# Two steps per batch taken off VectorE: the residual add goes to ScalarE and GpSimd, the sort offsets to TensorE

## The chip, the cores and the metric

One core of one Trainium2 chip runs the whole program. The metric is device time in microseconds (us) of one launch; the time of a kernel is the median of its runs. Five engines work side by side and meet only at semaphores: TensorE (PE; its weight loads are PEld), VectorE (DVE), ScalarE (ACT), GpSimd (POOL) and SyncE (SP), which here only issues DMAs. Each engine executes its own instructions in the order in which the program lists them.

## The reference, cut to what matters

The input is x of shape (8, 512, 128): 8 batches of 512 tokens. The block computes

```
x = layernorm(x + attention(x) @ Wo)     # 16 heads, differential, causal, RMS per head
x = layernorm(x + experts(x))            # 8 experts; each token goes to one of them
```

The attention of a batch needs softmax over 512 keys for 32 query heads of 4 values. Routing: `logits = x @ router_w + router_b`; a token goes to the expert of the largest logit, `y = (silu(a) * g) @ w2[e]`, and y is scaled by the largest softmax probability. The change touches two places: the sum `x + attention(x) @ Wo` ahead of the first layer norm, and the arithmetic that turns a token's expert and its rank among that expert's tokens into a row number.

## The kernel before, in words

**Phases.** The attention runs in 34 phases g = 0 to 33, four per batch (`SUPER` = 4, two of the eight key heads each). A phase has 9 slots t, each with two units u = 2t and 2t + 1. In a unit, TensorE makes scores for two uses: of phase g the block whose row maxima are wanted (VectorE reduces it, `row_max`, line 1396), and of phase g - 2 the turned block, which ScalarE exponentiates (line 963) and TensorE multiplies with v (`pv`, line 756). At the end of a phase VectorE folds the maxima (`pair_max`, lines 1405 and 1406); GpSimd splits them into three bf16 parts (`split_max`, lines 1141 to 1147, the first thing of its next phase); TensorE turns them (`turn_max`, line 793, slot 2 of the next phase), and they reach a later phase by DMA.

**Banks.** Scores and all small products go through two rings of PSUM banks: three banks emptied by VectorE (`nat_b`, semaphore `s_nfree`) and four emptied by ScalarE (`st_b`, `s_sfree`). Which ring a named product uses is told by `FOR_DVE` (line 122). In the last phases, products of batch 7 use an eighth bank.

**The chain of a batch.** Behind the attention of batch b comes a chain whose steps are placed by hand in tables: `CHAIN` gives for TensorE, ScalarE and GpSimd a phase (4b + lag) and a slot, `JOBS` for VectorE a phase and a unit from which one step follows each unit. In order: GpSimd forms the difference of the heads (`over_total`, `difference`, phase 4b + 6), `square`, `inverse_root` and `rms_norm` (4b + 7), `turn_attn` (4b + 8), the product with Wo (`wo`, 4b + 9, slot 8), VectorE's residual add from the bank into `res` (line 1417), six steps `stats` on VectorE (lines 1433 and 1439), `layer_norm` on GpSimd (lines 1224 to 1229, 4b + 10, slot 3), `turn_x1` (4b + 10, slot 8), `router` (4b + 11, slot 2, line 818), `choose` on VectorE, `rank` on TensorE (lines 824 to 833, 4b + 12), `place` on VectorE (lines 1481 to 1486), and `sort` on GpSimd: four indirect DMAs that scatter the tokens to `x_sorted` (line 1241). Every engine takes its entries in program order, so the steps of different batches that fall in one phase stand in line behind each other. In phases 4b + 10, GpSimd has in this order: `split_max`, four `split` steps of the keys of batch b + 3 (lines 1124 to 1130), `layer_norm(b)`, `over_total(b + 1)` and `difference(b + 1)`; then follows `split_max` of the next phase.

**Batch 6** is the exception: `CHAIN_SHORT` and `JOBS_SHORT` press its chain into phases 32 and 33; all six of its `stats` steps are done at unit 9 of phase 32. Phase 32 also holds the `place` steps of batch 5, from unit 8 on. `jobs_at` (line 142) yields the jobs of one unit by rising batch. The last step of `place` of batches 5 and 6 also runs `group(0)` and `group(1)` (line 1510): some twenty dependent little instructions that give the experts and rows of the slots of the second part; SP waits on them for the expert weights (`s_es`) and the rows (`s_base`), and for the scattered tokens (`s_scat`).

**The second part** (after phase 33): 23 slots of up to 256 sorted tokens each, `turn_x`, `hidden`, `down` on TensorE, with `take_x`, `gate` and `mix` on VectorE; batch 7's chain is woven in between.

Of the kernel before, what the change touches and what calls it, by code (L numbers as in the profile page):

```python
# [12 lines left out]
ALU = mybir.AluOpType  # L13
# [91 lines left out]
def outs_before(j, par):  # L105
# [15 lines left out]
BATCH_USES = [(6, "q", -4), (8, "q2", -4), (2, "k", -3), (6, "k2", -3), (2, "v", -2)]  # L121
FOR_DVE = ("wo", "router", "rank")

# [12 lines left out]

JOBS = {"guess": (7, 8, 3), "stats": (9, 17, 6), "choose": (11, 6, 8), "chance": (12, 0, 2),
        "place": (12, 8, 3)}
JOBS_SHORT = {"stats": (8, 9), "choose": (9, 7), "chance": (9, 12), "place": (9, 13)}
# [41 lines left out]


def rings():

    nat, st, nat_out, st_out = {}, {}, 0, 0
    nat_at, st_at = [], []
    for g in range(PHASES):
        for t in range(NC):
            if g < NS:
                for u in (2 * t, 2 * t + 1):  # L190
                    nat["max", g, u] = len(nat_at)
                    nat_out += 1
                    nat_at.append(nat_out)
            if 0 <= g - LAG < NS:
                for u in (2 * t, 2 * t + 1):
                    st["exp", g - LAG, u] = len(st_at)
                    st_out += 1
                    st_at.append(st_out)
            for name, n in uses(g, t):
                if name in FOR_DVE:  # L200
# [14 lines left out]
def build(nc, xT, x, wq, wv, wo, lam, rms, router_w, router_b, w12, c_rope, c_sign, c_ident, c_mask, c_tri, c_iota,  # L215
          c_rows, c_pad, out):
    with ExitStack() as ctx:
# [6 lines left out]
        def sem(name):  # L224
            return ctx.enter_context(nc.semaphore(name))
# [13 lines left out]
        mask_h, turned_h = (bits[:, 2 + 2 * i:4 + 2 * i, :].rearrange("p h (n t) -> p h n t", n=2) for i in range(2))  # L239
        tri = sb("tri", [P, 2, P], BF16)  # L240
        iota = sb("iota", [P, 4 * 16 + 2 * NX + NX * NX + 5 * 16 + SLOT // P + 1 + NTILE])
# [207 lines left out]
        s_rs2 = sem("s_rs2")  # L449
        s_norm = sem("s_norm")  # L450
        s_last = sem("s_last")
        s_outs = [sem("s_outs0"), sem("s_outs1")]
# [3 lines left out]

        RT_STEPS = 12

# [14 lines left out]
        def place(name, n):  # L473

            if (name, n) in TAIL_NO:
                return pv_b, s_tail, TAIL_NO[name, n], s_tfree
            if name in FOR_DVE:
                return nat_b[NAT_NO[name, n] % NAT_RING], s_nat, NAT_NO[name, n], s_nfree
            return st_b[ST_NO[name, n] % ST_RING], s_st, ST_NO[name, n], s_sfree

        def emptied(eng, name, n):

            if (name, n) in TAIL_NO:
                eng.wait_ge(s_tfree, TAIL_NO[name, n] + 1)
            elif name in FOR_DVE:
                eng.wait_ge(s_nfree, NAT_OUT[NAT_NO[name, n]])
            else:
                eng.wait_ge(s_sfree, ST_OUT[ST_NO[name, n]])

        def batch_of(g, lag):  # L490
# [4 lines left out]
        def over(a, shape, axis):  # L495
# [12 lines left out]
                  (rw_s[:, :], router_w), (rb_s[:, :], router_b.partition_broadcast(P)),  # L508
                  (tri[:, :, :], c_tri), (iota[:, :], c_iota),
                  (row_u[:, :, :].rearrange("p j a -> p (j a)"), c_rows)]  # L510
# [43 lines left out]
        def _(sp):  # L554
# [33 lines left out]
            for g in range(PHASES):  # L588
# [16 lines left out]
                for b in range(B - 1):  # L605
                    if g == SUPER * b + (CHAIN_SHORT if b == B - 2 else CHAIN)["wo"][0] + 1:

                        emptied(sp, "wo", b)
                        sp.dma_start(xn[:, :, :], x[(b + 1) * T:(b + 2) * T, :].rearrange("(i p) d -> p i d", p=P))\
                            .then_inc(s_xn, 16)  # L610
# [50 lines left out]
        def _(pe):  # L661
# [121 lines left out]
            def use(name, n):  # L783
                bk, done, no, _ = place(name, n)
                if (name, n) in TAIL_NO:
                    wait(pe, s_tfree, no)
                elif name in FOR_DVE:
                    nat_wait(pe, no)
                else:
                    st_wait(pe, no)  # L790
# [30 lines left out]
                elif name == "rank":  # L821
# [3 lines left out]
                    for i in range(NI - 1):  # L825
                        shape = [P, NI - 1 - i, NX]
                        m = pe.matmul(own[:, i + 1:NI, :], tri[:, 1, :], over(chosen[:, n % 2, i, :], shape, 1),
                                      start=False, stop=True, skip_group_check=True)
                    if n:
                        m = pe.matmul(own, tri[:, 1, :], over(cnt[:, n, :], [P, NI, NX], 1), start=False, stop=True,  # L830
                                      skip_group_check=True)
# [117 lines left out]
        def _(act):  # L949
# [25 lines left out]
            def take(name, n):  # L975
                if name in FOR_DVE:
                    return
# [16 lines left out]
                elif name == "turn_attn":  # L994
                    if n:
                        emptied(act, "wo", n - 1)
                    dst, src = dt_s[:, :], bk[:, :]
                elif name[0] in "qk":
                    a, cols = "qk".index(name[0]), HALF[len(name) - 1]
                    wait(act, s_split[a], 4 * n)  # L1000
                    dst, src = rot[:, a, cols], bk[:, cols]
                else:
                    if n:
                        emptied(act, "router", n - 1)
                    dst, src = x1t[:, :], bk[:, :]
# [90 lines left out]
        def _(pool):  # L1096
# [112 lines left out]
            def rms_norm(b):  # L1209
                wait(pool, s_newton, NEWTON * (b + 1))  # L1210
                wait(pool, s_post, 4 * b + 3)
                if b:
# [3 lines left out]
                    .then_inc(s_post, 1)  # L1216

            def layer_norm(b):

# [30 lines left out]
            for g in range(PHASES):  # L1250
                for t in range(NC):
# [20 lines left out]
                    if b is not None and t == 6:  # L1272
                        rms_norm(b)
                    b = chain_at("norm", g, t)
                    if b is not None:
# [51 lines left out]
        def _(dve):  # L1327
# [80 lines left out]
            def take(name, n):  # L1408
                if name not in FOR_DVE:
                    return  # L1410
# [12 lines left out]
                else:  # L1423
                    if n in GROUP_BATCH:
                        V.tensor_copy(total[:, n - GROUP_BATCH[0], :], bk[:, NI * NX:NI * NX + NX]).then_inc(s_total, 1)
                    V.tensor_tensor(coded[:, :, :], bk[:, 0:NI * NX].rearrange("p (i e) -> p i e", i=NI),
                                    over(io_region, BT, 1), ALU.add).then_inc(free, 1)

            def stats(b, k):

                if k < NI:
                    emptied(dve, "wo", b)
                    V.bn_stats(bst[:, k, :], res[:, k, :]).then_inc(s_bn, 1)
# [42 lines left out]
            def place_of(b, k):  # L1476

                wait(dve, s_rt, RT_STEPS * b + 10 + k)
                if k == 0:
                    emptied(dve, "rank", b)  # L1480
                    V.tensor_tensor(place_f[:, :, :], coded[:, :, :], chosen[:, b % 2, :, :], ALU.mult)\
                        .then_inc(s_rt, 1)
                elif k == 1:
                    V.tensor_reduce(pos_f[:, :], place_f[:, :, :], AX.X, ALU.add).then_inc(s_rt, 1)
# [360 lines left out]
```

## Time and profile before

| | us |
|---|---|
| median of 3 runs | 613.77 |
| the runs | 612.7, 620.75, 613.77 |
| profiled execution, its own time | 616.7 |
| its span, first to last instruction | 614.8 |
| PE busy | 566.8 (92% of the span) |
| DVE busy | 503.3 (82%) |
| ACT busy | 427.4 (70%) |
| POOL busy | 336.6 (55%) |
| mean granted TensorE clock | 0.950 |

The span leaves out 1.9 us of the execution's own time. Busy times of different engines overlap; a share is a mean over the attention phases and the second part, which have different limits. All the times given below are positions or lengths in this one execution.

### The profile page before, as it was taken

What the parts mean: (1) busy time and instruction counts of PE and PEld (TensorE: products, weight loads), DVE (VectorE), ACT (ScalarE), POOL (GpSimd) and SP (SyncE); (2) the same over time, 40 slices, a digit from 0 to 9 for tenths busy, and PEclk for the clock granted to TensorE, in tenths of its full rate; (3) what the DMA queues carried; (4) which work ended last, traced back from release to release, by engine and by line L of the source; (5) the groups of instructions that cost most, each with busy time, mean ns of one, the idle gap of its engine ahead of it and who ended that gap; (6) DMA issues with size and microseconds to landing.
All of it is one profiled execution on the core that took longest, in us unless ns stands there. A gap on an engine that the chain in (4) does not pass through costs nothing.

```text
span 614.8 us, 30825 instructions
## 1 busy us (share of the span) xinstructions
PE 566.8 (92%) x12925; PEld 341.1 (55%) x12925; DVE 503.3 (82%) x1251; ACT 427.4 (70%) x898; POOL 336.6 (55%) x573
## 2 busy tenths in 40 slices
PE   5499999999999999999999999999999797999992
PEld 1245454445554554455455445545555586999992
DVE  4477998998998999899989989999975688766673
ACT  3104888988887898888788888988888425444441
POOL 5322033772677397647748673842755216655584
PEclk9555899999999999999999999999999899999997
DMA  3603313321431342134124313312105682778510
GB/s 109 184 5 109 99 35 85 101 60 33 110 93 52 94 108 58 51 86 119 37 79 105 86 52 83 104 34 55 45 9 191 184 291 74 262 251 281 197 53 22
DMA packets 44083, 62.85 MB, mean 102 GB/s; under 512 B 13436, under 2 KB 35196, under 8 KB 43800
## 3 DMA queue, kind: packets, MB, share of 16 engines
q1 hardware_dynamic: 38888, 54.31, 30.2%
q0 software_dynamic: 2416, 5.08, 2.3%
q8 instruction: 102, 1.67, 1.2%
q10 hardware_dynamic: 2640, 1.48, 0.9%
q14 instruction: 37, 0.30, 0.2%
HBM read 42.79 MB, written 21.65 MB: 105 GB/s over the span
## 4 chain that ended last, share of the span: by engine, by line
PE 47%; DVE 22%; POOL 16%; issue 6%; DMA 4%; ACT 2%; SPq 0%; POOLq 0%; DVEq 0%; ACTq 0%
DVE mr L1396 15%; PE bank L756 10%; PE bank L892 8%; PE bank L689 7%; PE bank L671 6%; PE bank L907 3%; PE bank L767 3%; POOL x_all L1229 3%; PE bank L773 3%; PE bank L809 1%; PE bank L799 1%; PE bank L708 1%; DMA x_sorted<-x_all,pos_u 1%; POOL dif L1175 1%; POOL rstd L1226 1%
## 5 line engine op out<-in xcount | busy, mean ns | idle before, releaser
L1396 DVE TENSOR_REDUCE mr<-bank 128x8 f32<-128x512 f32 x576 | 363.0, 681 | 45.1 <-PE bank L689 42.5
L963 ACT ACTIVATE work<-bank 128x512 f32<-128x512 f32 x576 | 313.8, 600 | 54.8 <-PE bank L708 48.3
L756 PE MATMUL bank<-work,v_aug 128*32 128x256 f32 (+6 forms) x2560 | 172.5, 368 | 0.3 <-issue 0.3
L689 PE MATMUL bank<-kd,qd 24*64 24x192 bf16 (+7 forms) x2048 | 171.0, 295 | 0.0
L708 PE MATMUL bank<-qd,kd 27*64 27x320 bf16 (+7 forms) x2048 | 160.2, 286 | 0.0
L671 PEld LDWEIGHTS bank<-bits 32*64 32x64 bf16 x4608 | 79.3, 105 | 142.3 <-DVE mr L1396 65.3
L671 PE MATMUL bank<-bits 32*64 32x64 bf16 (+2 forms) x4608 | 134.2, 212 | 21.6 <-DMA kd<-qk_parts 10.7
L756 PEld LDWEIGHTS bank<-work,v_aug 128*32 128x32 f32 x2560 | 62.8, 109 | 57.7 <-issue 21.2
L1141 POOL CAST msplit<-mt 128x32 bf16<-128x32 f32 x32 | 6.7, 210 | 119.4 <-DVE mt L1406 119.4
L689 PEld LDWEIGHTS bank<-kd,qd 24*64 24x64 bf16 x2048 | 69.2, 111 | 0.0
L708 PEld LDWEIGHTS bank<-qd,kd 27*64 27x64 bf16 x2048 | 65.6, 108 | 0.1
L1076 ACT ACTIVATE sa<-bank 128x256 f32<-128x256 f32 (+1 forms) x92 | 30.4, 348 | 37.5 <-PE bank L892 29.0
L1241 POOL DMA_INDIRECT x_sorted<-x_all,pos_u x32 | 31.7, 992 | 27.0 <-DVE pos_u L1486 19.2
L1288 POOL DMA_INDIRECT out_dram<-ynorm,row_u x39 | 39.4, 1011 | 10.3 <-issue 8.8
L1111 POOL TENSOR_TENSOR xr<-xt_s,rope 128x512 f32<-128x512 f32 x28 | 34.7, 1271 | 9.7 <-DMA xt_s<-in_xT 9.7
L1726 DVE TENSOR_TENSOR u_s<-sa,bank 128x256 f32<-128x256 f32 (+1 forms) x92 | 32.3, 375 | 9.3 <-ACT sa L1076 8.6
L892 PE MATMUL bank<-xr,work 128*128 128x256 f32 (+1 forms) x192 | 37.2, 347 | 2.6 <-DVE xr L1682 2.5
L892 PE MATMUL bank<-xr,wbuf 128*128 128x256 f32 (+1 forms) x176 | 37.2, 365 | 1.3 <-DVE xr L1682 1.1
L892 PEld LDWEIGHTS bank<-xr,work 128*128 128x128 f32 x192 | 31.2, 191 | 6.0 <-DVE xr L1682 3.0
L1065 ACT ACTIVATE ynorm<-ymix,shift,rstd 128x128 f32<-128x128 f32 x37 | 16.5, 486 | 24.9 <-DMA out_dram<-ynorm,row_u 15.3
L892 PEld LDWEIGHTS bank<-xr,wbuf 128*128 128x128 f32 x176 | 30.3, 197 | 5.4 <-DVE xr L1682 1.7
L1298 POOL TENSOR_TENSOR rstd<-var,half 128x2 f32<-128x2 f32 (+1 forms) x23 | 15.5, 672 | 24.1 <-DVE var L1708 23.7
(203 smaller groups left out, 714.1 us busy)
## 6 DMA issues: line engine op xcount, KB each, us to landing
qk_parts<-parts SPq DMA_DIRECT2D x91, 128.0 KB, 2.6
work<-in_w SPq DMA_DIRECT2D x12, 768.0 KB, 6.3
wbuf<-in_w SPq DMA_DIRECT2D x11, 768.0 KB, 6.1
kd<-qk_parts SPq DMA_DIRECT2D x64, 96.0 KB
qd<-qk_parts SPq DMA_DIRECT2D x62, 96.0 KB
x_sorted<-in_c_pad SPq DMA_DIRECT2D x9, 390.0 KB, 4.3
xr<-x_sorted SPq DMA_DIRECT2D x16, 130.0 KB, 2.6
xt_s<-in_xT SPq DMA_DIRECT2D x8, 256.0 KB, 3.8
```

The source lines that it names most:

```text
L671: pe.matmul(bk[L * c:L * c + L, :].rearrange("p (n t) -> p n t", t=L)[:, first:first + step * (wide - 1) + 1:step, cols], unit_h[lo:lo + L ...
L689: m = pe.matmul(bk[L * c:L * c + L, cols], qd[lo:lo + KROWS, s % 2, second, c, L * n:L * n + L], kd[lo:lo + KROWS, s % 2, second, c, 0:key ...
L708: m = pe.matmul(bk[L * c:L * c + L, cols], kd[lo:lo + KROWS + MAXROWS, s % 2, second, c, L * n:L * n + L], qd[lo:lo + KROWS + MAXROWS, s % ...
L756: m = pe.matmul(pv_b[32 * t:32 * t + 32, lo:hi], v_aug[:, vb, kv + v, kb, :], prob[:, pos, r, lo - back:hi - back], start=piece == 0, stop ...
L892: m = pe.matmul(banks[f][:, h * SLOT:h * SLOT + P * WIDE[j]], w_slots[j % WRING][:, h * FFN + f * P:h * FFN + (f + 1) * P], xst[:, n % 2, ...
L963: nc.scalar.activation(prob[:, pos, r, :], st_b[no % ST_RING][:, :], ACT.Exp, scale=HD ** -0.5).then_inc(s_sfree, 1)
L1076: nc.scalar.activation(sa[:, f, 0:P * WIDE[j]], banks[f][:, 0:P * WIDE[j]], ACT.Silu).then_inc(s_silu, 1)
L1111: nc.gpsimd.tensor_tensor(xr[:, i, :], xt_s[:, :], rope[:, i, :], ALU.mult).then_inc(s_xr, 1)
L1241: nc.gpsimd.indirect_dma_start(out=x_sorted, out_offset=bass.IndirectOffsetOnAxis(pos_u[:, n:n + 1], 0), in_=x1_all[:, n, :], in_offset=None)\
L1288: nc.gpsimd.indirect_dma_start(out=out, out_offset=bass.IndirectOffsetOnAxis(row_u[:, j, a:a + 1], 0), in_=ynorm[:, j % 2, a, :], in_offse ...
L1396: V.tensor_reduce(mr[:, s % 2, u % 2, i, i:i + NB], nat_b[no % NAT_RING][:, :].rearrange("p (n t) -> p n t", t=L), AX.X, ALU.max)\
L1726: V.tensor_tensor(u_s[:, j % 2, f, 0:cols], sa[:, f, 0:cols], banks[f][:, SLOT:SLOT + cols], ALU.mult)\
```

## The change: what it does

For batches 0 to 5 the bank of the product with Wo belongs to ScalarE's ring instead of VectorE's. ScalarE copies it to `res` (128x512 f32), and GpSimd then adds `xn` to `res` in place (`add_x`, in phase 4b + 9, slot 8). SP's load of the next `xn` and VectorE's `stats` wait on the new semaphore `s_res`. The six `stats` steps of a batch begin four units later (from unit 17 of phase 4b + 9 to unit 3 of phase 4b + 10). Batches 6 and 7 keep VectorE's add.

In the ranks, one more small product on TensorE adds the region offset of each expert, so that the bank holds the whole row number; VectorE multiplies the bank by the flags `chosen` in the step that empties it. The separate addition of `io_region` goes, `place` has two steps instead of three, and `RT_STEPS` is 11 instead of 12. The constant `tri` becomes 8 columns wider.

```diff
-FOR_DVE = ("wo", "router", "rank")
+FOR_DVE = ("router", "rank")
...
-JOBS = {"guess": (7, 8, 3), "stats": (9, 17, 6), "choose": (11, 6, 8), "chance": (12, 0, 2),
-        "place": (12, 8, 3)}
+JOBS = {"guess": (7, 8, 3), "stats": (10, 3, 6), "choose": (11, 6, 8), "chance": (12, 0, 2),
+        "place": (12, 8, 2)}
...
+def for_dve(name, n):
+    return name in FOR_DVE or name == "wo" and n >= B - 2
...
+        def whole(eng, b):
+
+            if for_dve("wo", b):
+                emptied(eng, "wo", b)
+            else:
+                eng.wait_ge(s_res, b + 1)
...
-                        emptied(sp, "wo", b)
+                        whole(sp, b)
...
+                    m = pe.matmul(own, tri[:, 1, :], over(regions, [P, NI, NX], 1), start=False, stop=True,
+                                  skip_group_check=True)
...
+                elif name == "wo":
+
+                    wait(act, s_x1, 4 * n)
+                    dst, src = res[:, :, :], bk[:, :].rearrange("p (i d) -> p i d", i=NI)
...
+            def add_x(b):
+                emptied(pool, "wo", b)
+                wait(pool, s_xn, 16 * (b + 1))
+                nc.gpsimd.tensor_tensor(res[:, :, :], res[:, :, :], xn[:, :, :], ALU.add).then_inc(s_res, 1)
...
+                    b = chain_at("wo", g, t)
+                    if b is not None and not for_dve("wo", b):
+                        add_x(b)
...
-                    V.tensor_tensor(coded[:, :, :], bk[:, 0:NI * NX].rearrange("p (i e) -> p i e", i=NI),
-                                    over(io_region, BT, 1), ALU.add).then_inc(free, 1)
+                    V.tensor_tensor(place_f[:, :, :], bk[:, 0:NI * NX].rearrange("p (i e) -> p i e", i=NI),
+                                    chosen[:, n % 2, :, :], ALU.mult).then_inc(free, 1)
...
                 if k < NI:
-                    emptied(dve, "wo", b)
+                    whole(dve, b)
...
                     emptied(dve, "rank", b)
-                    V.tensor_tensor(place_f[:, :, :], coded[:, :, :], chosen[:, b % 2, :, :], ALU.mult)\
-                        .then_inc(s_rt, 1)
-                elif k == 1:
                     V.tensor_reduce(pos_f[:, :], place_f[:, :, :], AX.X, ALU.add).then_inc(s_rt, 1)
                 else:
                     V.tensor_copy(pos_u[:, NI * b:NI * b + NI], pos_f[:, :]).then_inc(s_pos, 1)
```

## Rows read from the trace of the kernel before

**Rows 1.** Windows, one batch: length; busy PE, PEld, DVE, ACT, POOL; clock, DMA, GB/s.

```profile
212.33:267.44 55.11, 53.33 (x1533) 28.45 (x1537) 50.56 (x107) 46.74 (x95) 36.49 (x63) 1.00 0.29 78
```

**Rows 2.** Chain that ended last, 214 to 219 us: start, length, what.

```profile
214.68 0.24 POOL msplit L1147
...
218.72 0.24 POOL vare L1224
```

**Rows 3.** Timeline of PE at slot 2 of phase 15: start, length, what, [idle before].

```profile
229.65 0.23 PE L793 MATMUL bank<-bits,msplit 128*96 128x128 bf16 x1 [0.17 <-POOL msplit L1147]
```

**Rows 4.** Timeline of DVE, 212 to 231 us.

```profile
212.33 0.69 DVE L1417 TENSOR_TENSOR res<-bank,xn 128x512 f32<-128x512 f32 x1
...
213.65 0.68 DVE L1396 TENSOR_REDUCE mr<-bank 128x8 f32<-128x512 f32 x1
...
217.35 0.24 DVE L1439 BATCH_NORM_AGGREGATE bag<-bst 128x2 f32<-128x6 f32 x2
217.50 3.05 DVE L1396 TENSOR_REDUCE mr<-bank 128x8 f32<-128x512 f32 x5
...
230.94 0.19 DVE L1421 TENSOR_TENSOR logit<-bank,rb_s 128x32 f32<-128x32 f32 x1 [0.19 <-PE bank L818]
```

**Rows 5.** Timeline of ACT, then of POOL, where phase 14 begins.

```profile
213.56 2.21 ACT L963 ACTIVATE work<-bank 128x512 f32<-128x512 f32 x4 [1.42 <-PE bank L708]
...
213.79 0.21 POOL L1141 CAST msplit<-mt 128x32 bf16<-128x32 f32 x1 [9.47 <-DVE mt L1406]
```

**Rows 6.** Groups by line and form: busy us, mean ns, idle before.

```profile
L1175 POOL TENSOR_TENSOR dif<-at 128x512 f32<-128x512 f32 x7 | 8.9, 1268 | 0.5
...
L1006 ACT ACTIVATE dt_s<-bank 128x512 f32<-128x512 f32 x8 | 4.8, 602 | 2.9 <-PE bank L803 2.9
```

**Rows 7.** Timeline of DVE (two `place` multiplications), then of PE behind the first.

```profile
244.05 0.18 DVE L1426 TENSOR_TENSOR coded<-bank,iota 128x32 f32<-128x32 f32 x1
...
246.34 0.98 DVE L1481 TENSOR_TENSOR place_f<-coded,chosen 128x32 f32<-128x32 f32 x1
...
412.16 0.18 DVE L1481 TENSOR_TENSOR place_f<-coded,chosen 128x32 f32<-128x32 f32 x1
...
247.98 0.25 PE L671 MATMUL bank<-bits 32*64 32x128 bf16 x3 [0.32 <-DVE mr L1396]
248.68 0.28 PE L671 MATMUL bank<-bits 32*64 32x128 bf16 x8 [0.19 <-DVE mr L1396]
```

**Rows 8.** Timeline of POOL, then of PE, batch 5 (phases 30 and 31).

```profile
435.01 0.23 POOL L1224 TENSOR_SCALAR vare<-bag 128x4 f32<-128x4 f32 x1 [2.75 <-DVE bag L1439]
...
445.94 0.23 PE L793 MATMUL bank<-bits,msplit 128*96 128x128 bf16 x1
```

**Rows 9.** Timeline of DVE, phases 32 and 33 and the start of the second part.

```profile
463.53 0.87 DVE L1433 BATCH_NORM_STATS2 bst<-res 128x6 f32<-128x128 f32 x4
...
464.85 0.29 DVE L1514 TENSOR_TENSOR above<-total,iota 128x128 f32<-128x128 f32 x1
...
468.94 0.17 DVE L1539 SCALAR_TENSOR_TENSOR used<-left,full 128x8 f32<-128x8 f32 x1
...
482.34 0.20 DVE L1543 CAST pad_i<-pad_f 128x8 int32<-128x8 f32 x1
484.33 0.42 DVE L1682 COPY xr<-bank 128x256 f32<-128x256 f32 x1 [1.79 <-PE bank L879]
```

**Rows 10.** Timeline of POOL, then of PE, same stretch.

```profile
464.97 0.25 POOL L1224 TENSOR_SCALAR vare<-bag 128x4 f32<-128x4 f32 x1 [6.18 <-DVE bag L1439]
...
469.76 0.63 PE L814 MATMUL bank<-ident,x_all 128*128 128x128 f32 x4 [0.98 <-POOL x_all L1229]
483.89 0.30 PE L879 MATMUL bank<-ident,xr 128*128 128x128 f32 x1 [2.48 <-DMA xr<-x_sorted]
```

**Rows 11.** Chain that ended last: the scatter of batch 5 under way.

```profile
473.75 6.82 DMA x_sorted<-x_all,pos_u
```

**Rows 12.** Windows: granted clock (PEclk) after TensorE's idle stretch before 483.89.

```profile
486.00:488.00 2.00, 2.00 (x6) 1.53 (x6) 2.00 (x5) 0.86 (x2) 0.00 (x0) 0.50 0.89 261
```

More of the change, by code:

```diff
@@ L199, in rings @@
             for name, n in uses(g, t):
-                if name in FOR_DVE:
+                if for_dve(name, n):
                     nat[name, n] = len(nat_at)
@@ L239, in build @@
         mask_h, turned_h = (bits[:, 2 + 2 * i:4 + 2 * i, :].rearrange("p h (n t) -> p h n t", n=2) for i in range(2))
-        tri = sb("tri", [P, 2, P], BF16)
+        tri_s = sb("tri_s", [P, 2 * P + NX], BF16)
+        tri = tri_s[:, 0:2 * P].rearrange("p (a m) -> p a m", a=2)
+        regions = tri_s[:, 2 * P:]
         iota = sb("iota", [P, 4 * 16 + 2 * NX + NX * NX + 5 * 16 + SLOT // P + 1 + NTILE])
@@ L450, in build @@
         s_norm = sem("s_norm")
+        s_res = sem("s_res")
         s_last = sem("s_last")
@@ L454, in build @@
         block = ctx.enter_context(nc.Block())
-        RT_STEPS = 12
+        RT_STEPS = 11
         def wait(eng, s, n):
@@ L476, in place @@
                 return pv_b, s_tail, TAIL_NO[name, n], s_tfree
-            if name in FOR_DVE:
+            if for_dve(name, n):
                 return nat_b[NAT_NO[name, n] % NAT_RING], s_nat, NAT_NO[name, n], s_nfree
@@ L484, in emptied @@
                 eng.wait_ge(s_tfree, TAIL_NO[name, n] + 1)
-            elif name in FOR_DVE:
+            elif for_dve(name, n):
                 eng.wait_ge(s_nfree, NAT_OUT[NAT_NO[name, n]])
@@ L508, in build @@
                   (rw_s[:, :], router_w), (rb_s[:, :], router_b.partition_broadcast(P)),
-                  (tri[:, :, :], c_tri), (iota[:, :], c_iota),
+                  (tri_s[:, :], c_tri), (iota[:, :], c_iota),
                   (row_u[:, :, :].rearrange("p j a -> p (j a)"), c_rows)]
@@ L786, in use @@
                     wait(pe, s_tfree, no)
-                elif name in FOR_DVE:
+                elif for_dve(name, n):
                     nat_wait(pe, no)
@@ L975, in take @@
             def take(name, n):
-                if name in FOR_DVE:
+                if for_dve(name, n):
                     return
@@ L1408, in take @@
             def take(name, n):
-                if name not in FOR_DVE:
+                if not for_dve(name, n):
                     return
@@ L1832 @@
         "c_mask": np.concatenate([np.eye(P)[:, None], unit, causal, turned], 1).astype(ml_dtypes.bfloat16),
-        "c_tri": np.stack([before, np.ones((P, P), f)], 1).astype(ml_dtypes.bfloat16), "c_iota": iota,
+        "c_tri": np.concatenate([before, np.ones((P, P), f), np.broadcast_to(np.arange(NX, dtype=f) * (REGION // P), (P, NX))],
+                                1).astype(ml_dtypes.bfloat16),
+        "c_iota": iota,
         "c_rows": spare.astype(np.uint32),
```

## The prediction, on record before the changed kernel ran

> **What bounds the kernel now.** I read the page first, for the shares of the engines, then the windows of one batch, then the chain that ended last through that batch, and the timelines at its joints. The page invites a wrong conclusion: TensorE 92% busy, VectorE 82%, so work taken from VectorE should shorten the attention. The windows of a batch say the same: in 55.11 us VectorE is busy 50.56, GpSimd only 36.49 [rows 1]. The reader is to see in the chain that it isn't so evenly spread. From 214.68 to 229.65 the chain is GpSimd and nothing else: the split of the maxima, the four key splits, `layer_norm` from 218.72 [rows 2], the two steps of the next batch's difference, and the next split of the maxima, whose end releases TensorE's `turn_max`. TensorE had waited 0.17 us for it [rows 3], and behind it in TensorE's order stands the router product, for which VectorE in turn waited 0.19 us [rows 4]. The start of GpSimd's queue is released by the maxima [rows 5]. So in phases 4b + 10 GpSimd has no slack: it is full for 15 us, and its last piece gates TensorE, VectorE and ScalarE together, once per batch. In the other three phases TensorE and VectorE limit each other, and GpSimd has room; the 9.47 us of idle time before phase 14 are the largest hole [rows 5]. The windows hide this, being a mean over all four.
>
> **Part 1, the residual add.** VectorE loses one instruction of 0.69 us in each of six batches [rows 4]: 4.1 us busy. How much of it was on the path? Before row maximum 0 of the new phase VectorE needs a bank that TensorE fills only after the Wo product and one `pv` step. The first exponential of the phase waits 1.42 us for the same TensorE stretch and starts at 213.56, while VectorE starts at 213.65 [rows 4, 5]. So the add lies in a hole: without it VectorE would start at about 213.55. With one bank less in its ring the Wo product may start some 0.1 to 0.3 us sooner. I take 0.25 us for both together, between 0.1 and 0.4.
>
> ScalarE gains a copy like that of `dt_s`, 0.60 us [rows 6], in the same 1.42 us hole: hidden. If that hole were gone it would cost up to 0.6. GpSimd gains an add of 128x512 with both inputs in SBUF, as in `difference`: 1.27 us [rows 6]. It can start when ScalarE's copy ends, about 212.8, and ends near 214.1, so `split_max` is issued about 0.3 us later than at 213.79 [rows 5]. Queued behind it are the key splits and `layer_norm`. That alone would delay the GpSimd chain by 0.3 us.
>
> **Part 2, the later stats, which is the term that decides.** `layer_norm` needs both aggregate steps. They ended at 217.59, more than 1 us before GpSimd was ready at 218.72: slack [rows 2, 4]. Now they end after unit 8 instead of unit 4: four more row maxima at (3.05 - 0.68) / 4 = 0.59 to 0.61 us each, 2.42 us [rows 4]. All six steps now fall behind row maximum 0, one more than before, 0.19 us. Less the 0.25 us of the earlier start: 217.59 + 2.42 + 0.19 - 0.25 = 219.95. GpSimd, free at 219.0, stands idle until then; `layer_norm` starts at 219.98 instead of 218.72, 1.26 us later, and everything behind it moves with it, to `turn_max` and the router product. Nothing absorbs it, since TensorE was already waiting there [rows 3] and VectorE behind it [rows 4]. Per batch I take +1.3 us, between 0.9 and 1.8 (the upper end if TensorE can't feed VectorE at that pace in this phase). Five batches, 0 to 4: +6.5.
>
> In batch 5 there are no key splits ahead of `layer_norm`, which already waited 2.75 us for the aggregates [rows 8]. The whole shift counts: 2.42 + 0.19 - 0.25 = 2.36. `turn_max` ran at 445.94 with no wait listed, but the split had ended only 0.14 before, so little is absorbed: +2.2.
>
> **Part 3, the ranks.** In the full phases the multiplication `place_f` took 0.98 us, against 0.18 us in batch 4, when GpSimd was idle; four batches (0 to 3) show about 1.0. The step that reads its first operand from the bank took 0.18 us, while GpSimd was busy in the same way [rows 7]. The new multiplication reads the bank too, so I take 0.18, no more than it replaces, and 0.98 us goes from VectorE in four batches. Behind it TensorE had waited 0.32 and 0.19 us [rows 7]; after that it is TensorE's turn, so I count 0.5 of the 0.98 per batch, between 0 and 0.9: -2.0. The extra product on TensorE is a 32-column one among four such, under 0.1 us.
>
> The Trainium skill, "SBUF — State Buffer", section "Who interferes with whom", says that a VectorE instruction with two SBUF inputs and a GpSimd instruction that reads SBUF block each other for a whole instruction. If that held also for the new GpSimd add, VectorE would have to run such an instruction beside it; in its 1.3 us stand only row maxima and the folded maxima, with one input each, and the sum doesn't change.
>
> **Part 4, an order that changes unseen.** In phase 32 `place` of batch 5 begins at unit 8. Before, its last step, with `group(0)`, fell on unit 10, after the six stats steps of batch 6 at unit 9: the trace shows the stats from 463.53 and then the group from 464.85 to 469.11 [rows 9]. With two steps instead of three the last one falls on unit 9, and `jobs_at` yields batch 5 before batch 6. So the group's 4.26 us and the cast of the row numbers ahead of it now stand ahead of the stats of batch 6: about +4.4 us for them. `layer_norm(6)` waited for exactly these, from 464.97, and TensorE waited 0.98 us for its output at 469.76 [rows 10]; the four scatters of batch 5 stand behind it in GpSimd's queue, the last from 473.75, and the first slot's tokens wait for them [rows 10, 11]. What is the path into the second part? VectorE's `group(1)` ended at 482.54 and its first `take_x` began at 484.33, held by the scatter's landing [rows 9, 10]. With everything 4.4 us later the group ends at 486.9, so `take_x` runs at 486.9: +2.6. The scatter is 4.4 us later in its start, but it took 6.82 us [rows 11] while the weights that wait for the same group were loading; those loads now start about 1.2 us earlier (the group no longer waits for the stats) and the scatter later, so it may be shorter. Whether it binds lies between 2.6 and 4.4. I take 2.6. TensorE stands idle for some 5 us in phase 33. After the idle stretch before 483.89 the granted clock was 0.50 for a while, the lower of its two levels [rows 12]; that may come earlier now, or come twice: 1.5 us either way, in the range only.
>
> **Sum.** +6.5 + 2.2 - 2.0 + 2.6 = +9.3 us. The profiled execution would take 616.7 + 9.3 = 626.0. It is 2.9 above the median, and by the median, 613.8 + 9.3 = 623.1.
>
> **The rivals.** (A) VectorE's relief counts: the stats are no later for GpSimd than its splits let it notice, because row maxima run faster than I think once the add is gone, and group(0) doesn't hold up the tail. For it speaks the 82% share of VectorE; against it its waits at the joint [rows 3, 4]. It would save 6 x 0.25 + 4 x 0.5 = 3.5 us at least and 4.1 + 4 x 0.8 = 7.3 at most: 606 to 610. The Trainium skill, "Perfetto Trace Analysis", section "Optimizing Scalar/DVE Operations", holds that with a saturated VectorE it may pay to offload to ScalarE or even GpSimd; by that rule this is the outcome, which the chain [rows 2] speaks against. (B) The same mechanism at its upper bounds, slower than now by over 2%: 5 x 1.8 + 2.4 + 4.4 + 1.5, nothing back from part 3: +17, 631. It decides if the scatter's landing binds and TensorE starves VectorE in phase 4b + 10; the point beyond which it is over 2% is +12.3. (C) The main phases as I say, but the tail absorbs part 4 (or the weights' earlier start pays for it): +6.7 or less, 620. (D) The change does nothing that is seen: the stall at `turn_max` is offset by shorter waits later in the batch, as when the pipeline catches up: 611 to 616. Against it: after the router product all three engines start from an empty ring, as before.
>
> **Chances.** My forecast 0.55, C 0.15, B 0.13, D 0.09, A 0.08. A spread of 2% is what a measurement of this kernel can tell from no change (12.3 us). Only B lies beyond it on the slow side, with a little of my forecast's upper edge; only an A beyond its bounds on the fast side. Range: A and half of D are left out below, the top of B above: 614.5 to 628.5.
>
> **What would show it.** GpSimd's first `layer_norm` instruction waits for `bag` in all of batches 0 to 4 (0.9 us), where it waited in batches 5 and 6 alone; `turn_max` in phases 4b + 11 waits 1 to 1.5 us for `msplit`; a batch lasts about 55.9 us instead of 55.1; no multiplication of 1 us is left in `place`; the group's instructions stand ahead of the stats of batch 6, and TensorE's `turn_x1` of that batch waits some 5 us. The forecast is wrong if `bag` is ready by 219.0 in the terms of batch 1, if `turn_max` shows no longer wait, or if the second part starts at the same distance from phase 32 as before.

## The result, and the profile after

| | before | after |
|---|---|---|
| median, us (lowest to highest, runs) | 615.38 (612.7 to 620.75, 4 runs) | 634.25 (629.18 to 636.33, 4 runs) |
| ratio after / before, 95% interval | | 1.0276 [1.0229, 1.0323] |
| profiled execution, its span | 616.7, 614.8 | 636.33, 634.5 |
| mean granted TensorE clock | 0.950 | 0.922 |

Slower, by 18.9 us; the forecast was 9.3 us. Executions of one kernel fall into a faster and a slower state; the ratios here and below are estimated from the faster ones alone, the medians and ranges from all, so that a ratio is not the quotient of two medians.

Two lines of the page of after, the busy time and share of each engine, and the granted clock (tenths of 2.4 GHz) in 40 slices of the span:

```profile
PE 577.2 (91%) x12933; PEld 344.4 (54%) x12933; DVE 496.5 (78%) x1237; ACT 431.8 (68%) x904; POOL 344.5 (54%) x579
...
PEclk9555899999989999999999999899987599999997
```

VectorE is 6.8 us less busy, as meant, and TensorE 10.4 us more, though it got only one tiny product more per batch: the same work ran at a lower clock. The slices show where: dents in the attention (slices 12, 26 and 30), and 7, 5 at slices 31 and 32.

The fixed points of both traces are the starts of the Wo products; "Wo 5" is that of batch 5, and a time such as +9.07 is counted from the start of the batch's own Wo product. They split the 19.7 us by which the span grew:

| stretch | before | after | difference | predicted |
|---|---|---|---|---|
| start to Wo product of batch 0 | 156.01 | 156.65 | +0.64 | 0 |
| Wo 0 to Wo 5 (`turn_max` of batches 0 to 4) | 272.46 | 279.40 | +6.94 | +4.5 |
| Wo 5 to Wo 6 (that of batch 5) | 33.24 | 37.39 | +4.15 | +2.2 |
| Wo 6 to Wo 7 (phase 33, start of the second part) | 36.20 | 44.30 | +8.10 | +2.6 |
| Wo 7 to the end | 116.89 | 116.76 | -0.13 | 0 |

The joint of batch 1, which answers to [rows 2 to 5]. In before its Wo product starts at 211.14; timeline of TensorE:

```profile
211.14 1.16 PE L809 MATMUL bank<-wo_n,dt_s 128*128 128x128 f32 x8
```

Timeline of GpSimd in after; then of VectorE; then of TensorE:

```profile
215.46 1.27 POOL L1241 TENSOR_TENSOR res<-res,xn 128x512 f32<-128x512 f32 x1 [8.98 <-ACT res L1026]
216.67 0.21 POOL L1161 CAST msplit<-mt 128x32 bf16<-128x32 f32 x1
...
222.66 0.23 POOL L1249 TENSOR_SCALAR vare<-bag 128x4 f32<-128x4 f32 x1 [1.14 <-DVE bag L1467]
```

```profile
216.04 2.48 DVE L1424 TENSOR_REDUCE mr<-bank 128x8 f32<-128x512 f32 x4 [0.61 <-PE bank L703]
...
222.33 0.24 DVE L1467 BATCH_NORM_AGGREGATE bag<-bst 128x2 f32<-128x6 f32 x2
...
234.92 0.19 DVE L1449 TENSOR_TENSOR logit<-bank,rb_s 128x32 f32<-128x32 f32 x1 [1.69 <-PE bank L832]
```

```profile
213.59 1.16 PE L823 MATMUL bank<-wo_n,dt_s 128*128 128x128 f32 x8
...
233.63 0.23 PE L807 MATMUL bank<-bits,msplit 128*96 128x128 bf16 x1 [1.66 <-POOL msplit L1167]
```

Read it from the Wo product on. The aggregates end 8.98 us after it, where they had ended 6.45 after it [rows 4]; `layer_norm` starts at +9.07 instead of +7.58 [rows 2] and waits 1.14 us for them; `turn_max` runs at +20.04 instead of +18.51 and waits 1.66 us instead of 0.17 [rows 3]. This wait stands in all of batches 0 to 5, at 1.65 to 1.67 us. GpSimd's new add lasts 1.27 us and is itself hidden. Up to here it is the predicted chain.

What was not predicted is the line below the joint. Windows of after: the batch, then 2 us of it behind `turn_max`:

```profile
213.59:270.01 56.42, 53.58 (x1536) 28.35 (x1531) 49.32 (x106) 47.44 (x96) 37.81 (x64) 0.97 0.26 74
235.00:237.00 2.00, 2.00 (x72) 0.74 (x57) 1.59 (x5) 1.09 (x2) 1.33 (x4) 0.50 0.39 109
```

TensorE is full and ScalarE half empty at a granted clock of 0.50 (1.2 GHz). The clock falls so behind `turn_max` in every batch but batch 2, where it stays at 1.00 with the same wait of 1.66 us. From Wo 2 to Wo 3, at full clock, it took 55.78 us, which is the 55.9 of the prediction; from Wo 0 to Wo 1, with a fall, 56.94.

The tail, answering to [rows 9, 10]. Timeline of VectorE, then of TensorE, then windows of after:

```profile
475.21 0.28 DVE L1539 TENSOR_TENSOR above<-total,iota 128x128 f32<-128x128 f32 x1
...
479.05 0.17 DVE L1564 SCALAR_TENSOR_TENSOR used<-left,full 128x8 f32<-128x8 f32 x1
479.25 0.87 DVE L1461 BATCH_NORM_STATS2 bst<-res 128x6 f32<-128x128 f32 x4
```

```profile
485.44 1.09 PE L828 MATMUL bank<-ident,x_all 128*128 128x128 f32 x4 [4.93 <-POOL x_all L1254]
489.45 2.08 PE L832 MATMUL bank<-rw_s,x1t 128*128 128x128 f32 x8
504.87 0.44 PE L895 MATMUL bank<-ident,xr 128*128 128x128 f32 x2
```

```profile
473.44:517.74 44.30, 38.17 (x451) 23.15 (x450) 22.65 (x97) 22.44 (x45) 12.30 (x14) 0.77 0.54 178
...
486.00:488.00 2.00, 2.00 (x19) 0.72 (x17) 0.00 (x0) 0.60 (x1) 1.56 (x2) 0.50 0.98 401
...
502.00:504.00 2.00, 2.00 (x22) 0.80 (x18) 0.83 (x5) 0.18 (x1) 1.42 (x2) 0.50 0.11 33
```

The group stands ahead of the stats of batch 6, and `turn_x1` of that batch waits 4.93 us instead of 0.98. The clock falls within this wait and stays at 0.50 from 486 to 504, though TensorE is busy all that time. The router product takes 2.08 us there, 1.13 at full clock.

### The profile page after: what moved, and what is told of

Read it like the earlier page. It is cut to its first block, busy times and chain, and to the rows that moved or that the text cites. A ratio compares the mean times of both kernels' runs of the same rounds, so it can differ in the third digit from the quotient of the medians.

```text
span 634.5 us, 30845 instructions
## 1 busy us (share of the span) xinstructions
PE 577.2 (91%) x12933; PEld 344.4 (54%) x12933; DVE 496.5 (78%) x1237; ACT 431.8 (68%) x904; POOL 344.5 (54%) x579
## 3 DMA queue, kind: packets, MB, share of 16 engines
q8 instruction: 102, 1.67, 1.1%
## 4 chain that ended last, share of the span: by engine, by line
PE 53%; DVE 23%; POOL 12%; issue 6%; DMA 3%; ACT 2%; POOLq 0%; SPq 0%; DVEq 0%; ACTq 0%
DVE mr L1424 14%; PE bank L770 13%; PE bank L703 8%; PE bank L685 7%; PE bank L908 7%; POOL x_all L1254 3%; PE bank L923 3%; PE bank L781 3%; PE bank L787 2%; PE bank L813 2%; PE bank L722 2%; PE bank L832 2%; PE bank L823 1%; POOL dif L1195 1%; POOL rstd L1251 1%
## 5 line engine op out<-in xcount | busy, mean ns | idle before, releaser
L770 PE MATMUL bank<-work,v_aug 128*32 128x256 f32 (+6 forms) x2560 | 179.3, 382 | 0.0
L685 PE MATMUL bank<-bits 32*64 32x64 bf16 (+2 forms) x4608 | 132.4, 216 | 19.6 <-DMA kd<-qk_parts 11.6
L1241 POOL TENSOR_TENSOR res<-res,xn 128x512 f32<-128x512 f32 x6 | 7.6, 1272 | 55.1 <-ACT res L1026 55.1
L908 PE MATMUL bank<-xr,wbuf 128*128 128x256 f32 (+1 forms) x176 | 35.4, 353 | 1.3 <-DVE xr L1707 1.3
```

The lines of the kernel that those rows point to most:

```text
L685: pe.matmul(bk[L * c:L * c + L, :].rearrange("p (n t) -> p n t", t=L)[:, first:first + step * (wide - 1) + 1:step, cols], unit_h[lo:lo + L ...
L770: m = pe.matmul(pv_b[32 * t:32 * t + 32, lo:hi], v_aug[:, vb, kv + v, kb, :], prob[:, pos, r, lo - back:hi - back], start=piece == 0, stop ...
L908: m = pe.matmul(banks[f][:, h * SLOT:h * SLOT + P * WIDE[j]], w_slots[j % WRING][:, h * FFN + f * P:h * FFN + (f + 1) * P], xst[:, n % 2, ...
```

## The experiments

Two questions: do the two orders (stats behind unit 3, group ahead of the stats of batch 6) carry the loss, and how much of each loss is the order itself (the wait, at full clock), how much the lower clock behind it? In two experiments TensorE gets extra products whose results nothing reads; they only fill its idle time. "Before" beside these runs had medians of 617.1 (first four), 618.01 (next four) and 615.49 (the last); the ratios are each to its own.

**1. The place of the group put right.**

```diff
-        "place": (12, 8, 2)}
+        "place": (12, 9, 2)}
```

> The changed kernel with the two place steps one unit later (unit 9 and 10), so that in phase 32 the six stats steps of batch 6 again stand ahead of group(0). Theory T1 (the tail's 8.0 us come from the swapped order: 4.3 us of dependent instructions ahead of the stats, and the half clock that TensorE's long wait brings on in phase 33): the wait of turn_x1 of batch 6 falls from 4.93 us to about 1, phase 33 runs at clock 1.00, and the whole is 7 to 8.5 us shorter, about 626. Rival R1 (the tail is longer for another reason, the order being hidden behind the weight loads): less than 2 us shorter, 632 to 634.

Measured: 627.13 us (623.16 to 629.76), ratio 1.0164 [1.0062, 1.0266], span 625.3. In its timelines of VectorE and of TensorE the stats of batch 6 come first again, and its window from Wo 6 to Wo 7 is at full clock:

```profile
476.15 0.87 DVE L1461 BATCH_NORM_STATS2 bst<-res 128x6 f32<-128x128 f32 x4
...
477.46 0.28 DVE L1539 TENSOR_TENSOR above<-total,iota 128x128 f32<-128x128 f32 x1
```

```profile
482.37 0.63 PE L828 MATMUL bank<-ident,x_all 128*128 128x128 f32 x4 [0.97 <-POOL x_all L1254]
```

```profile
474.33:508.56 34.23, 30.02 (x452) 20.05 (x450) 23.03 (x98) 22.10 (x45) 12.31 (x14) 1.00 0.65 209
```

One unit in a table gives 10.1 us in this stretch (44.30 to 34.23), 7.1 in the median. The two differ in part because the profiled executions do: in this one Wo 0 to Wo 5 takes 282.26 us, 2.9 more than in after with the same waits of 1.66 us, as the clock stays low for longer behind them in batches 0 and 1. What a fall of the clock costs is thus not the same in each execution.

**2. The stats two units earlier.**

```diff
-JOBS = {"guess": (7, 8, 3), "stats": (10, 3, 6), ...
+JOBS = {"guess": (7, 8, 3), "stats": (10, 1, 6), ...
```

> The changed kernel with the stats steps two units earlier, from unit 1 of phase 4b + 10. Theory T1 (layer_norm's start is set by the last stats step, and what stands behind it gates turn_max): layer_norm waits 0 to 0.2 us instead of 1.14, turn_max 0.4 to 0.7 us instead of 1.66, the clock no longer falls behind it in most batches; six batches by 1.1 us plus what the clock took: 8 to 11 us shorter, about 624 to 626. Rival R2 (GpSimd's add in front of the queue is what delays the chain, 1.2 us of its own): layer_norm can't start sooner, turn_max still waits about 1.6 us, within 1 us of the changed kernel.

Measured: 621.41 us (618.76 to 624.59), ratio 1.0078 [1.0037, 1.012], span 622.3. Timeline of GpSimd, then of TensorE, and the window of batch 1:

```profile
218.19 0.23 POOL L1249 TENSOR_SCALAR vare<-bag 128x4 f32<-128x4 f32 x1
```

```profile
229.16 0.23 PE L807 MATMUL bank<-bits,msplit 128*96 128x128 bf16 x1 [0.85 <-POOL msplit L1167]
```

```profile
210.17:265.04 54.87, 53.29 (x1537) 28.41 (x1531) 49.37 (x106) 47.29 (x96) 37.95 (x64) 1.00 0.27 75
```

`layer_norm` waits no longer, `turn_max` waits 0.85 us in this batch (0.4 to 0.7 expected), and behind it the clock stays at 1.00 in every batch. The gain, 12.8 us in the median, is more than the 8 to 11 expected. The tail is as in after (44.43 us from Wo 6 to Wo 7).

**3. Both.**

> Both edits together, place from unit 9 and stats from unit 1. T1: the gains add up, 15 to 19 us less than the changed kernel, 616 to 619, level with the kernel before within 1%. If the relief of VectorE is worth what its busy time says (rival A of the prediction), it would now show: 606 to 610.

Measured: 613.74 us (611.93 to 616.88), ratio 0.9945 [0.9902, 0.9989], span 611.6, clock 0.950. With both orders mended the whole loss is gone, where 616 to 619 was expected, and the change is about 0.5% faster than before (0.1 to 1.1%).

**4. Extra products in phase 33, wrong order kept.**

```diff
+                        if (name, n) == ("turn_x1", B - 2):
+                            fill(place("router", n)[0], NAT_NO["router", n], 22)
```

`fill` issues 22 products of 128x512 bf16 into the router's bank, which the router product then overwrites.

> The changed kernel with 22 products of 128x512 bf16 (about 4.7 us, their result is overwritten) on TensorE in phase 33 ahead of turn_x1 of batch 6, in the time in which it only waits. The order of place and stats stays as changed. Theory T1 says that of the tail's 8.0 us about 4.4 are the group's instructions and the rest is the half clock of phase 33: the wait stays, the granted clock stays at 1.00, and the whole is 3 to 5 us shorter. Rival R3 (the clock costs nothing there, since ScalarE and the dependences set the pace): within 1 us of the changed kernel though the clock is 1.00.

Measured: 629.59 us (626.12 to 637.61), ratio 1.0203 [1.0072, 1.0334], span 625.2. The median is 4.7 us below that of the whole change (3 to 5 expected), but the interval of its ratio overlaps the other's, 1.0229 to 1.0323; what the experiment shows stands in the trace. Timeline of TensorE and the window from Wo 6 to Wo 7:

```profile
477.65 4.92 PE L800 MATMUL bank<-kd,bits 128*128 128x512 bf16 x22
482.66 0.63 PE L833 MATMUL bank<-ident,x_all 128*128 128x128 f32 x4
484.88 1.16 PE L837 MATMUL bank<-rw_s,x1t 128*128 128x128 f32 x8
```

```profile
470.65:507.04 36.39, 34.94 (x474) 22.03 (x472) 22.66 (x97) 22.13 (x45) 12.30 (x14) 1.00 0.62 201
```

`turn_x1` is as late as in after (12.01 us behind Wo 6, against 12.00), yet the stretch takes 36.39 us instead of 44.30. The late order itself costs 2.4 us (36.39 against 33.97 in experiment 5, both at full clock); 7.9 us are the clock in this pair of executions. Experiments 8 and 9 will show the same wait with a stretch of 39.83 and 39.96 us, where the clock takes some 3.5.

The path into the second part is the one of the prediction. In this run `take_x`, 24.51 us behind Wo 6, follows `group(1)` on VectorE without a wait, and TensorE waits no longer for the scattered tokens, for which it waited 2.48 us before [rows 10]: the scatter does not bind. Timeline of VectorE:

```profile
495.04 0.20 DVE L1575 CAST pad_i<-pad_f 128x8 int32<-128x8 f32 x1
495.16 0.41 DVE L1714 COPY xr<-bank 128x256 f32<-128x256 f32 x1
```

**5. The ranks alone**, on the kernel before, with the stats where they were, VectorE's residual add kept, and `place` at (12, 9, 2).

```diff
-        "place": (12, 8, 3)}
+        "place": (12, 9, 2)}
...
+                    m = pe.matmul(own, tri[:, 1, :], over(regions, [P, NI, NX], 1), start=False, stop=True,
+                                  skip_group_check=True)
...
-                    V.tensor_tensor(coded[:, :, :], bk[:, 0:NI * NX].rearrange("p (i e) -> p i e", i=NI),
-                                    over(io_region, BT, 1), ALU.add).then_inc(free, 1)
+                    V.tensor_tensor(place_f[:, :, :], bk[:, 0:NI * NX].rearrange("p (i e) -> p i e", i=NI),
+                                    chosen[:, n % 2, :, :], ALU.mult).then_inc(free, 1)
```

> The kernel before with the rank part alone (region offsets by TensorE, multiplication out of the bank, place in two steps from unit 9, so that the group stays behind the stats of batch 6); VectorE keeps the residual add. Theory T2 (of VectorE's relief only this part is on the path, 0.5 us in each of the four batches whose multiplication took 1 us): 1.5 to 3.5 us faster than before, batches 0 to 3 last 54.4 to 54.7 us instead of 55.1. Rival R4 (the gain of the kernel with both repairs came from the moved add as well): less than 1 us here, batches of 55.0 us.

Measured: 613.19 us (609.3 to 620.2), ratio 0.9904 [0.9862, 0.9946], span 609.8. Timeline of VectorE, and the windows of batch 1 and from Wo 6 to Wo 7:

```profile
244.61 0.18 DVE L1430 TENSOR_TENSOR place_f<-bank,chosen 128x32 f32<-128x32 f32 x1
```

```profile
211.74:265.89 54.15, 53.10 (x1530) 28.60 (x1530) 49.59 (x107) 46.51 (x96) 36.62 (x63) 1.00 0.28 76
458.90:492.87 33.97, 30.16 (x451) 20.04 (x450) 23.02 (x98) 22.10 (x45) 12.29 (x14) 1.00 0.65 206
```

The fastest version of the study by its ratio, though its interval and that of experiment 3 overlap: it takes the gain and leaves the residual add where it was. A batch takes 54.13 to 54.21 us, 0.96 less than before. 2.2 us more come from the clock at the start of the second part, which before fell to 0.60 and 0.54 in the windows from 485 to 489 and here stays at 1.00. TensorE waits for the scattered tokens there in both (2.48 and 2.19 us), so that these 2.2 us may be luck of the execution.

**6. The later stats alone**, on the kernel before: `"stats": (10, 3, 6)` and nothing else.

> The kernel before with one table entry changed: stats from unit 3 of phase 4b + 10; VectorE keeps the residual add, nothing is moved to ScalarE or GpSimd. Theory T1 (the late stats steps are what costs in the attention phases): layer_norm waits about 1.3 us in batches 0 to 4, turn_max 1.3 to 1.9 us, and the kernel is 8 to 13 us slower than before though no work was added. Rival R2 (GpSimd's added work is the cost): within 2 us of before.

Measured: 633.53 us (631.12 to 636.19), ratio 1.0276 [1.0204, 1.0349], span 630.3. The ratio of the whole change, from one table entry. Timeline of GpSimd, then of TensorE, of VectorE and once more of GpSimd, and a window behind `turn_max`:

```profile
223.42 0.23 POOL L1224 TENSOR_SCALAR vare<-bag 128x4 f32<-128x4 f32 x1 [1.88 <-DVE bag L1439]
```

```profile
234.38 0.31 PE L793 MATMUL bank<-bits,msplit 128*96 128x128 bf16 x1 [1.66 <-POOL msplit L1147]
```

```profile
252.23 1.19 DVE L1481 TENSOR_TENSOR place_f<-coded,chosen 128x32 f32<-128x32 f32 x1
```

```profile
252.10 1.28 POOL L1111 TENSOR_TENSOR xr<-xt_s,rope 128x512 f32<-128x512 f32 x1
```

```profile
234.00:236.00 2.00, 1.62 (x8) 1.65 (x9) 0.00 (x0) 0.27 (x1) 1.92 (x3) 0.57 0.42 128
```

Its Wo product of batch 1 starts at 214.35, so `layer_norm` starts at +9.07 and `turn_max` at +20.03, to 0.01 us where they start in after. Here VectorE still does the residual add: its 0.69 us were worth nothing on this path. A batch takes 57.98 us.

The kernel is 15.5 us slower than before by the medians, more than the 8 to 13 expected, and it gets there on another way than the whole change: nothing is lost in phase 33 (33.95 us from Wo 6 to Wo 7), but Wo 0 to Wo 5 takes 286.07 us, 13.6 more than before. The order explains 6.2 of them (experiments 8 and 9); the other 7.4, by this difference, would be the clock, which here falls behind all six waits of 1.66 us. No run fills the waits of this kernel, so that this last share is an estimate.

**7. Experiment 3 with `turn_max` one slot later.**

```diff
-PAIR_USES = [(2, "turn_max", 1), (4, "turn_ot", 3)]
+PAIR_USES = [(3, "turn_max", 1), (4, "turn_ot", 3)]
```

> The changed kernel with both repairs (place from unit 9, stats from unit 1) and turn_max one slot later, slot 3, in every phase, so that TensorE has the router product and one more slot of scores to do before it needs GpSimd's split. If the gate at turn_max is what still costs 0.8 us per batch: no wait for msplit left in phases 4b + 11, batches of 53.6 to 54.0 us instead of 54.4, 3 to 5 us less than with both repairs alone, 608 to 611. Rival R5 (VectorE or ScalarE is next at once, the wait only moves): within 1 us of both repairs, 613 to 614.

Measured: 620.14 us (612.04 to 628.15), ratio 0.9983 [0.9929, 1.0038], span 614.9. The expected gain is not there. The waits at `turn_max` are gone and two batches take 53.76 us (54.41 in experiment 3), but the turned maxima reach the next phase later. From its waits by releaser (engine, line, total, times, longest), and the windows of batch 1 and inside it:

```profile
PE bank L685 <- DMA qd<-max_rows: 6.0, 4, 2.4
```

```profile
212.36:267.56 55.20, 54.09 (x1538) 28.57 (x1531) 49.21 (x106) 47.39 (x96) 37.81 (x64) 0.97 0.29 79
...
222.00:224.00 2.00, 2.00 (x50) 0.94 (x48) 0.94 (x2) 1.64 (x4) 2.00 (x3) 0.50 0.08 12
```

TensorE waits for that load instead (0.8 us in experiment 3), twice ahead of Wo 0. Wo 0 comes 3.4 us later (158.60 against 155.24), but how much of it these waits cost is open: experiments 5 and 9, whose programs are the same up to there, differ by 2.8 us (157.61 and 154.79). Batch 1 loses its gain to a dent in the clock. TensorE's matmuls wait no longer than 0.32 us at a time in that batch, so this dent has no cause that I can show.

**8. Extra products ahead of `turn_max`, on the changed kernel.**

```diff
+                    if n % SUPER == 2 and n >= 10:
+                        for _ in range(7):
+                            pe.matmul(bk[:, :], ident_b[:, :],
...
```

Seven products of 128x512 bf16 into the bank of `turn_max`, in the phases of its wait, before `turn_max` overwrites it.

> The changed kernel with 7 products of 128x512 bf16 (about 1.5 us, overwritten) on TensorE ahead of its wait in turn_max, in phases 4b + 11 of batches 0 to 5 alone, where it waits 1.66 us. Theory T1 with the clock as its second part: the stall stays, the granted clock no longer falls behind it; the windows behind turn_max are at 1.00, the six batches are together 3 to 5 us shorter, about 630; phase 33 is untouched and keeps its half clock. Rival R3 (the clock's fall after these stalls costs nothing): within 1 us of the changed kernel.

Measured: 626.96 us (625.38 to 633.08), ratio 1.0188 [1.011, 1.0266], span 624.7. Timeline of TensorE, and the window of batch 1:

```profile
230.94 1.46 PE L808 MATMUL bank<-bits 128*128 128x512 bf16 x6 [0.16 <-issue]
232.35 0.26 PE L811 MATMUL bank<-bits,msplit 128*96 128x128 bf16 x1
```

```profile
212.41:268.36 55.95, 54.69 (x1542) 28.93 (x1537) 49.33 (x106) 47.32 (x96) 37.91 (x64) 1.00 0.27 76
```

The trace has six of the seven products. `turn_max` is as late as in after (+19.94 against +20.04), with the clock at 1.00 behind it in all six batches. Wo 0 to Wo 5 takes 275.77 us instead of 279.40, Wo 5 to Wo 6 35.72 instead of 37.39. So 3.6 and 1.7 us of the loss there are the clock, again in this pair of executions (3 to 5 expected together).

**9. The ranks alone, at the change's own unit 8.**

```diff
-        "place": (12, 8, 3)}
+        "place": (12, 8, 2)}
```

> The rank part alone with the place that the change gives it: the kernel before with the ranks multiplied from the bank and two place steps begun at unit 8, so that the group of batch 5 stands ahead of the six stats of batch 6; VectorE keeps the residual add and the stats keep their place. T1 (the order in phase 32 costs what it cost in the changed kernel, whatever the attention phases do): the attention batches stay at 54.1 us as in the rank part begun at unit 9 (profile 609.8 us), turn_x1 of batch 6 waits 4.9 us for GpSimd instead of 0.97, the granted clock falls to 0.50 for 10 to 20 us in phase 33, and from the Wo product of batch 6 to that of batch 7 it takes 44 us instead of 33.97: span about 620, 618 to 623, ratio to before 1.00 to 1.015. T2 (the 8 us of the tail need the main phases' delay too, or the clock falls only after their low stretches): the wait of 4.9 us is there but the stretch takes no more than 38 to 39 us, span 613 to 615, ratio 0.99 to 1.00.

Measured: 621.14 us (616.26 to 622.29), ratio 1.0071 [1.0037, 1.0105]. The profiled execution, at 616.4, is among the three shortest of ten; the other seven lie between 619 and 622.3. Timeline of TensorE, the window from Wo 6 to Wo 7, and two windows in it:

```profile
469.62 1.09 PE L816 MATMUL bank<-ident,x_all 128*128 128x128 f32 x4 [4.93 <-POOL x_all L1233]
```

```profile
457.61:497.57 39.96, 33.68 (x451) 21.81 (x450) 22.66 (x97) 22.29 (x45) 12.24 (x14) 0.87 0.55 184
...
469.00:471.00 2.00, 1.38 (x12) 0.96 (x16) 0.00 (x0) 0.26 (x1) 1.59 (x2) 0.50 1.03 430
...
477.00:479.00 2.00, 2.00 (x40) 1.16 (x34) 0.68 (x4) 1.52 (x5) 0.00 (x0) 0.75 0.27 67
```

The wait of 4.93 us is T1's, so is the median; the profiled stretch, 39.96 us, lies between the theories. The same wait keeps the clock low for some 10 us here and in experiment 8 (39.83 us), and for some 20 us in after and in experiment 2 (44.30 and 44.43). How long does not follow from the wait, which is the same in all four; it may be a matter of the execution. That the longer executions of this kernel are the 20-us ones is likely from the 2 to 6 us between its times, but only one was profiled. Its batches take 54.53 us.

## Why the prediction was wrong in size, and where it was right

With experiments 4, 5, 8 and 9 the 19.7 us come apart into orders and clock. Each row is the difference between two profiled executions, one of each kernel. The rows of the orders are compared at full clock; those of the clock vary with the execution: the attention of experiment 1, with the waits of after, took 2.9 us more than that of after, and phase 33 of experiments 8 and 9, with the wait of after, 4.5 and 4.3 us less.

| term | predicted | measured | from |
|---|---|---|---|
| late stats, batches 0 to 4 (residual add in it) | +6.5 | +6.2 | Wo 0 to Wo 5, exp. 8 - exp. 9 |
| late stats, batch 5 | +2.2 | +2.4 | Wo 5 to Wo 6, exp. 8 - exp. 9 |
| ranks | -2.0 | -2.9 | Wo 0 to Wo 5, exp. 9 - before |
| group ahead of the stats | +2.6 | +2.4 | Wo 6 to Wo 7, exp. 4 - exp. 5 |
| small rests (start, end, batch 5) | 0 | +0.6 | |
| clock behind `turn_max` | 0 | +5.3 | after - exp. 8: 3.63 + 1.67 |
| clock in phase 33 and behind | 0 (1.5 either way) | +7.9 - 2.2 | after - exp. 4; before's own loss goes, exp. 5 - before |

The sum without the clock is +8.7, against a forecast of +9.3; the clock adds 11.0. **The step that failed is the last of part 4**, "1.5 us either way, in the range only", and that part 2 has no such term at all: it took the clock's loss as nothing. Six new TensorE waits of 1.66 us and one of 4.93 us were priced at their length. Five of the six and the long one were followed by a stretch at half clock in which TensorE, the engine that nearly everything waits for there, did the same work in up to twice the time. [Rows 12] showed the mechanism, behind a wait that the kernel before already had, and I used it only as a tremor of the range.

**Part 1 right that the add stands in a hole, wrong in its small gain.** VectorE's relief was taken at 0.25 us per batch, and it was not there; experiment 6 has the same `layer_norm` and `turn_max` times with VectorE's add as after has without it: 0 on this path. The copy and the add are hidden as said; `split_max` comes 3.08 us behind the Wo product instead of 2.65, 0.43 later (0.3 said). The move with its later stats costs a little even in the best order tried: experiment 3 against 5, which differ by both, has 54.41 us per batch against 54.15. No run has the move with the stats where they were, so its own share is open.

**Part 2 right**, in place and size: waits of 1.14 us for `bag` (0.9 said) and of 1.66 at `turn_max` (1 to 1.5 said). In batch 5 `layer_norm` started at +9.07 instead of +6.53, 2.54 us later (2.36 said). At full clock a late order costs 1.25 us per batch, the moved add in it (1.3 said).

**Part 3 right in sign.** The multiplication is 0.18 us, no more than the addition it replaces. 0.58 us per batch come back, and 0.96 when `place` begins one unit later, just above the upper end of "between 0 and 0.9"; why that unit matters no run shows. The Trainium skill, "SBUF — State Buffer", section "Who interferes with whom", says that a VectorE instruction with two SBUF inputs contends with a GpSimd instruction that reads SBUF. The rows agree: 0.98 to 1.01 us with both inputs in SBUF beside a busy GpSimd, 1.19 to 1.20 in experiment 6, 0.18 with one input in the bank beside the same GpSimd instruction. They also show why 0.98 in one kernel and 1.19 in the other. Timeline of GpSimd in before, beside the multiplication of [rows 7]:

```profile
246.01 1.28 POOL L1111 TENSOR_TENSOR xr<-xt_s,rope 128x512 f32<-128x512 f32 x1
```

GpSimd's instruction ends at 247.29 and the multiplication, begun at 246.34, at 247.32; in experiment 6 they end at 253.38 and 253.42. In both the multiplication lasts until GpSimd is done, and how long that is depends on when it begins.

**Part 4 right in order and in the cost of order**: `turn_x1` waits 4.93 us (some 5 said), and Wo 7 comes later by 2.4 at full clock (2.6 said for the start of the second part). That it is the group and not the scatter on which `take_x` waits was a choice in the prediction, and the right one (experiment 4).

Of the rivals, B came nearest in size (+17), but by luck: it put the path terms at their upper bounds, and these stayed at their middle. Its 1.5 us for the clock would have had to be 11. A is refuted as a forecast, and for the residual add altogether: VectorE is 6.8 us less busy and the kernel slower; only the ranks' part of the relief shows, in experiments 5 and 9. C is refuted by the 8.1 us that phase 33 lost, 2.4 of them at full clock, and D by the 1.25 us per batch that nothing later made up for. The Trainium skill, "Perfetto Trace Analysis", section "Optimizing Scalar/DVE Operations", says that offloading from a saturated VectorE may pay; VectorE, 82% busy, was not what the joint waited for, and for the residual add no run here shows a gain.

## What to carry to other kernels

Where the bounding engine is TensorE, a new wait of its own is not priced by its length: read in the trace before what the granted clock did behind waits like it, and give the work that follows a price at half clock as a case with its own chance. A shorter list of steps in a hand-written schedule moves its last step, and what hangs on that step, past its neighbours; write out the order on each engine before and after. Test a move's parts apart: here a part worth 5.0 us of span by itself (experiment 5; 2.2 of them the clock) was buried under two table entries worth 22.9 (after against experiment 3).

## What the runs showed of the hardware

- The granted clock fell at or behind waits of 1.64 to 1.67 us in five of six batches of after, in all six of experiments 1 and 6 and in four of six of experiment 4, but not in batch 2 of after with the same wait, nor behind waits of 0.81 to 0.85 us in experiment 2. The length of one wait alone doesn't decide it.
- The fall can come late and outlasts the wait: in after it was 0.50 over 235 to 237, with TensorE busy since 233.63, and in phase 33, where it fell within the wait, it stayed at 0.50 from 486 to 504, with TensorE back at work since 485.44 and busy for all of these 18 us.
- A fall can also come with no long wait ahead of it: 0.50 over 222 to 224 in experiment 7.
- The same wait of 4.93 us was followed by some 10 us at 0.50 in two executions and by some 20 in two others.
- Extra products whose results nothing reads, put into a wait, paid for themselves: 22 of them took 7.9 us off the stretch from Wo 6 to Wo 7 (44.30 to 36.39), and 7 ahead of each late `turn_max` took 5.3 off those from Wo 0 to Wo 6 (316.79 to 311.49).
